# A decoder layer's last gather: waiting for the last block that holds rows, and the last normalisation on three engines

## What is computed

```python
x = _layernorm(x + _L0_attn_ref(x, ...), axis=-1)
x = _layernorm(x + _L0_xattn_ref(x, itok_BxS_13_99985, ctx_2048, ctx_2048, ctx_2048), axis=-1)
x = _layernorm(x + _L0_ffn_ref(x, ...), axis=-1)

def _L0_ffn_ref(x, gate_w, w_gate, w_up, w_down, sw_gate, sw_up, sw_down, expert_bias):   # E, K = 16, 2
    logits = flat @ gate_w.T
    probs = jax.nn.softmax(logits, axis=-1)
    _, top_idx = jax.lax.top_k(logits + expert_bias, K)
    top_w = jnp.take_along_axis(probs, top_idx, axis=-1)
    top_w = top_w / jnp.sum(top_w, axis=-1, keepdims=True)
    ...
    for e in range(E):
        out = out + combine[:, e:e + 1] * _swiglu(flat, w_gate[e], w_up[e], w_down[e])
    out = out + _swiglu(flat, sw_gate, sw_up, sw_down)
```

## Time and profile before

| | us |
|---|---|
| median of 3 runs | 677.91 |
| lowest, highest | 677.41, 678.26 |
| span of the profiled execution | 680.0 |
| mean granted TensorE clock | 0.971 |
| PE, DVE, ACT, POOL busy | 636.0, 531.8, 447.2, 475.5 |

### The profile page before, as it was taken

The page is one execution under the profiler, slowest core; times in us unless marked ns, Lnnn a source line. Parts: engine busy times, 40 slices in busy tenths (PEclk is TensorE's granted clock), DMA queues, the critical chain, the costliest instruction groups (busy, mean ns, idle before and its releaser), DMA issues.

```text
span 680.0 us, 11968 instructions
## 1 busy us (share of the span) xinstructions
PE 636.0 (94%) x3544; PEld 493.4 (73%) x3544; DVE 531.8 (78%) x849; ACT 447.2 (66%) x723; POOL 475.5 (70%) x452
## 2 busy tenths in 40 slices
PE   7999999999999999999999999999999999899920
PEld 6677887888878878888788788788898776455510
DVE  6999999999999999999999999859754539222236
ACT  3768788788787887887878879875324445333321
POOL 5395988789879887798798887586805817655244
PEclk9999999999999999999999999999999969999965
DMA  4231113113111131121111311133062780587324
GB/s 157 107 134 48 65 47 109 62 47 109 58 50 62 47 109 62 47 105 53 59 62 47 109 62 46 37 96 107 24 171 78 190 329 4 169 257 200 88 89 128
DMA packets 25896, 65.08 MB, mean 96 GB/s; under 512 B 4051, under 2 KB 16851, under 8 KB 23131
## 3 DMA queue, kind: packets, MB, share of 16 engines
q1 hardware_dynamic: 23035, 56.96, 25.2%
q0 software_dynamic: 2832, 7.75, 4.4%
HBM read 56.42 MB, written 8.28 MB: 95 GB/s over the span
## 4 chain that ended last, share of the span: by engine, by line
PE 68%; DVE 15%; issue 6%; ACT 5%; POOL 4%; DMA 2%; POOLq 0%; DVEq 0%; ACTq 0%
PE ps L835 27%; DVE conv L1662 8%; PE ps L865 7%; PE ps L849 5%; PE ps L1129 5%; PE ps L767 3%; PE ps L785 3%; ACT decay L1330 3%; PE ps L1173 3%; DVE decay L1646 3%; PE ps L850 2%; PE ps L809 2%; POOL conv L706 2%; PE ps L1103 1%; PE ps L874 1%
## 5 line engine op out<-in xcount | busy, mean ns | idle before, releaser
L1662 DVE SCALAR_TENSOR_TENSOR conv<-ps,w_raw,conv 128x506 f32<-128x506 f32 (+3 forms) x352 | 320.9, 935 | 12.1 <-ACT conv L1324 7.2
L835 PE MATMUL ps<-x_hi,w_hi 128*128 128x512 f32 x384 | 158.1, 412 | 3.8 <-DVE conv L1662 2.0
L835 PE MATMUL ps<-x_hi,w_lo 128*128 128x512 f32 x384 | 151.1, 393 | 0.0
L835 PE MATMUL ps<-x_lo,w_hi 128*128 128x512 f32 x384 | 150.0, 391 | 0.0
L1324 ACT ACTIVATE conv<-ps,w_raw 128x512 f32<-128x512 f32 x160 | 108.1, 686 | 61.4 <-PE ps L835 61.2
L498 POOL TENSOR_TENSOR decay<-cum_b,cum_tok 128x512 f32<-128x512 f32 (+1 forms) x128 | 103.2, 828 | 9.0 <-DMA cum_b<-cum_scratch 9.0
L835 PEld LDWEIGHTS ps<-x_hi,w_hi 128*128 128x128 f32 x384 | 72.2, 188 | 21.4 <-DVE conv L1662 3.5
L504 POOL TENSOR_TENSOR decay<-decay,mask 128x512 f32<-128x512 f32 x64 | 82.4, 1288 | 5.0
L835 PEld LDWEIGHTS ps<-x_hi,w_lo 128*128 128x128 f32 x384 | 72.0, 188 | 16.8 <-DVE w_lo L1588 0.2
L849 PE MATMUL ps<-conv 128*128 128x256 f32 x256 | 79.6, 393 | 2.3 <-DVE xs L1637 0.4
L835 PEld LDWEIGHTS ps<-x_lo,w_hi 128*128 128x128 f32 x384 | 72.4, 189 | 12.7
(11 more groups left out here) (263 smaller groups left out, 1101.6 us busy)
## 6 DMA issues: line engine op xcount, KB each, us to landing
cum_b<-cum_scratch SPq DMA_DIRECT2D x16, 1024.0 KB, 4.7
w_raw<-in_winT SPq DMA_DIRECT2D x15, 778.0 KB, 4.3
y_all<-in_wgu SPq DMA_DIRECT2D x4, 1408.0 KB, 11.6
late<-in_wdn SPq DMA_DIRECT2D x2, 1408.0 KB
x_scratch<-conv SPq DMA_DIRECT2D x19, 128.0 KB, 4.6
late<-in_woutT SPq DMA_DIRECT2D x1, 2048.0 KB, 8.3
ys_scratch<-y_blk SPq DMA_DIRECT2D x32, 64.0 KB
res_scratch<-conv SPq DMA_DIRECT2D x11, 130.0 KB
```

The costliest lines, as they stand in the source:

```text
L835: mm = pe.matmul(ps[:, tile_bank(n, tile) + hf, :], wp[:, par, w], xp[:, kk, t], start=(i == 0), stop=(i == 5))
L1662: dve.scalar_tensor_tensor(out=o[:, :, s:], in0=u[:, :, 0:T - s], scalar=w_raw[:, par, c:c + 1], in1=o[:, :, s:], op0=ALU.mult, op1=ALU.ad ...
```

## The change

Six things change together.

- The tail's gathers are cut in four parts, in this order: first pick of tiles 0 to 2; second pick of tiles 0 and 1; first pick of tiles 3 to 7; second pick of tiles 2 to 7. In round 22 (`SEEN_AT`) DVE works out for each part the last block that holds one of its rows. PE turns that [128, 4] table in round 24 behind the transposes' wait of item 23, DVE takes its maximum and writes four numbers.
- SP waits for each store to land, block after block, and counts `y_seen` up (`landed`). For blocks 0 to 8 it does that after it has issued block 8's store. Before each part POOL loads the part's number into a register, waits for `y_seen` against it, and does a one-column sum.
- POOL's `gather_block` runs up to seven blocks ahead from block 16 on, and the residual gathers come after blocks 7 to 14.
- The weight copies move to other places in memory, so that the gathered rows' place is free early. One wait of SP goes. `ys_dram` is filled once, early, from `x` (three transfers, 1.5 MB).
- ACT makes the exponentials of the picks in round 25, between two table loads. DVE makes the weights in round 27, and does `weigh_low` of tiles 0 to 2 before `gate_block` of the last item. ACT takes the last two `take_hidden`.
- The last normalisation is done by ACT for tiles 0 to 2, by POOL for 3 to 5 (after its last gather), by DVE for 6 and 7 (after its last statistics). The weighted sums are made in place in `y_of`, so a tile no longer waits for the normalisation of the one two before.

```diff
+PICK_PARTS = ((0, 0, HOISTED), (1, 0, LEADING), (0, HOISTED, TB), (1, LEADING, TB))   # HOISTED, LEADING = 3, 2
@@ SP, early
             load_cum(1, 1)
+            for lo, hi in YS_SET:
+                sp.dma_start(ys_dram[lo * G:hi * G, :], x[0:(hi - lo) * G, :]).then_inc(S["ys_set"], 16)
@@ SP, expert loop
+            def landed(j):
+                sp.wait_ge(st_y[j % NW], stored(j))
+                sp.sem_inc(S["y_seen"], 1)
             for j in range(NBLK):
                 store_block(j)
                 if 1 <= j <= NCOPY:
                     load_copy(j - 1)
+                if j == NCOPY + 1:
+                    for d in range(j):
+                        landed(d)
+                if j > NCOPY:
+                    landed(j)
@@ POOL
-                if j >= AHEAD:
+                if j >= NBLK - NX:
+                    pool.wait_ge(S["tx_done"], j - NX + 1)
+                elif j >= AHEAD:
                     pool.wait_ge(S["tx_done"], j - AHEAD + 1)
-                if j >= 9 and j % 2 == 1 and j < 9 + 2 * TB:
-                    gather_res((j - 9) // 2)
+                if 7 <= j < 7 + TB:
+                    gather_res(j - 7)
+            pool.wait_ge(S["v_lb"], 1)
+            for n, (k, lo, hi) in enumerate(PICK_PARTS):
+                pool.wait_ge(S["y_seen"], pool.value_load(last_blk[n:n + 1, 0:1], min_val=1, max_val=NBLK))
+                pool.tensor_tensor(part_seen[:, n:n + 1], zero[:, :], zero[:, :], ALU.add)
+                for b in range(lo, hi):
+                    gather_row(k, b)
+            for b in range(LAST_ACT, LAST_POOL):
+                pool.wait_ge(S["q2"], b + 1)
+                pool.tensor_scalar(o_tok[:, b, :], y_of[:, 0, b, :], ln_m2[:, b, 0:1], ln_v2[:, 1, b:b + 1],
+                                   ALU.subtract, ALU.mult).then_inc(S["n2p"], 1)
@@ ACT
+                if i == PICK_AT:
+                    act.preload_act_table_set("natural_log_exp_and_others")
+                    act.wait_ge(S["ld_res"], 16 * TB)
+                    act.activation(e_pick, res_tok[:, :, D + 2:D + 4].rearrange("p b k -> p k b"), ACT.Exp).then_inc(S["a_el"], 1)
+                    act.preload_act_table_set("silu_and_others")
@@ DVE
+            for i in range(TBS, ITEMS):
+                if i == ITEMS - 1:
+                    for b in range(HOISTED):
+                        weigh_low(b)
+                gate_block(i)
+                if TBS < i < ITEMS - 1:
                     take_hidden(i - 1)
+                if i == SEEN_AT:
+                    blocks_of_picks()
+                if i == PICK_AT + 2:
+                    weights_of_picks()
             for b in range(TB):
+                weigh_high(b)
+                if b + HOISTED < TB:
+                    weigh_low(b + HOISTED)
+                if b == TB - 1:
+                    for c in range(LAST_POOL, TB):
+                        last_norm(c)
@@ DVE, new functions
+            def blocks_of_picks():
+                dve.wait_ge(S["ld_res"], 16 * TB)
+                vlink(dve.tensor_copy(slot_t.rearrange("p (k b) -> p k b", k=PICKS),
+                                      res_tok[:, :, D:D + 2].rearrange("p b k -> p k b")))
+                vlink(dve.tensor_scalar(seen_a, slot_t, 6, NE - 1, ALU.logical_shift_right, ALU.bitwise_and),
+                      dve.tensor_scalar(seen_b, slot_t, 7, None, ALU.logical_shift_right))
+                vlink(dve.scalar_tensor_tensor(out=seen_c, in0=seen_b, scalar=float(NE), in1=seen_b, op0=ALU.is_ge, op1=ALU.mult))
+                vlink(dve.tensor_tensor(seen_f.rearrange("p k b -> p (k b)"), seen_a, seen_c, ALU.max))
+                for n, (k, lo, hi) in enumerate(PICK_PARTS):
+                    dve.tensor_reduce(part_f[:, n:n + 1], seen_f[:, k, lo:hi], AX.X, ALU.max).then_inc(S["v_blk"], 1)
+            def weigh_high(b):
+                r = y_of[:, 0, b, :]
+                dve.wait_ge(ld_y[b], 16 if b < HOISTED else 32)
+                dve.wait_ge(S["v_mix"], b + 1)
+                vlink(dve.scalar_tensor_tensor(out=r, in0=y_of[:, 1, b, :], scalar=w_pick[:, 1, b:b + 1], in1=r, op0=ALU.mult, op1=ALU.add))
+                vlink(dve.bn_stats(ln_s[:, b % 2, :], r))
+                dve.bn_aggr(ln_m2[:, b, :], ln_s[:, b % 2, :]).then_inc(S["s2"], 1)
```

More of the change, by code:

```diff
@@ L217, in build_layer @@
         slot_t = take(PICKS * TB).bitcast(I32)
+        seen_a, seen_b, seen_c = (take(PICKS * TB).bitcast(I32) for _ in range(3))
+        seen_f = take(PICKS * TB).rearrange("p (k b) -> p k b", k=PICKS)
+        part_f, part_seen, part_top = (take(NPART) for _ in range(3))
+        last_blk = take(1).bitcast(I32)
         e_pick, w_pick = (take(PICKS * TB).rearrange("p (k b) -> p k b", k=PICKS) for _ in range(2))
@@ L1148, in turn_hidden @@
                     pe.wait_ge(S["v_ht"], i - 1 - TBS)
+                if i == SEEN_AT + 1:
+                    pe.wait_ge(S["v_blk"], NPART)
+                    pe.transpose(ps[0:NPART, i % 2, 2 * P:3 * P], part_f, ident[:, :])
                 for c in range(2):
@@ L1156, in down @@
                     pe.wait_ge(S["a_ht"], i + 1)
-                else:
+                elif i < ITEMS - 2:
                     pe.wait_ge(S["v_ht"], i - TBS + 1)
@@ L1160, in down @@
                         pe.wait_ge(S["ld_dn"], 32)
+                else:
+                    pe.wait_ge(S["a_ht"], TBS + i - (ITEMS - 2) + 1)
                 if i >= 2:
@@ L1561, in _ @@
                     take_y(TBS - 1)
-                if i - 2 >= TBS:
+                if i < ITEMS and i - 2 >= TBS:
+                    take_y(i - 2)
+                if i >= ITEMS:
+                    take_hidden(i - 2)
+                    if i == ITEMS:
+                        act.preload_act_table_set("natural_log_exp_and_others")
                     take_y(i - 2)
@@ L1760, in rlink @@
-            def rlink(*group):
-                for ins in group:
-                    made[0] += 1
-                    ins.then_inc(S["v_rt"], 1)
-                dve.wait_ge(S["v_rt"], made[0])
+                if b < HOISTED:
+                    dve.wait_ge(ld_row[NX + b], 32)
+                else:
+                    dve.wait_ge(ld_y[b], 32)
+                dve.scalar_tensor_tensor(out=y_of[:, 0, b, :], in0=y_of[:, 0, b, :], scalar=w_pick[:, 0, b:b + 1],
+                                         in1=res_tok[:, b, 0:D], op0=ALU.mult, op1=ALU.add).then_inc(S["v_mix"], 1)
@@ L1893, in _ @@
                 dve.wait_ge(S["a_lg"], c + 1)
-                rlink(dve.tensor_tensor(biased[:, lo:hi, 0:NE], logit[:, lo:hi, :],
+                vlink(dve.tensor_tensor(biased[:, lo:hi, 0:NE], logit[:, lo:hi, :],
                                         eb_sb.unsqueeze(1).broadcast_to([P, n, NE]), ALU.add))
-                rlink(*[dve.max(top8[:, b, :], biased[:, b, 0:NE]) for b in range(lo, hi)])
-                rlink(dve.memset(top8[:, lo:hi, 2:8], PAD))
-                rlink(*[dve.match_replace(out=taken[:, b, :], in_to_replace=top8[:, b, :],
+                vlink(*[dve.max(top8[:, b, :], biased[:, b, 0:NE]) for b in range(lo, hi)])
+                vlink(dve.memset(top8[:, lo:hi, 2:8], PAD))
+                vlink(*[dve.match_replace(out=taken[:, b, :], in_to_replace=top8[:, b, :],
                                           in_values=biased[:, b, :], imm_value=HIT) for b in range(lo, hi)])
@@ L1973, in take_hidden @@
                                 ).then_inc(S["v_ht"], 1)
-            for i in range(TBS, ITEMS + 1):
-                if i < ITEMS:
-                    gate_block(i)
-                if i > TBS:
-                    take_hidden(i - 1)
-                if i == ITEMS - 2:
-                    dve.wait_ge(S["ld_res"], 16 * TB)
-                    dve.tensor_copy(slot_t.rearrange("p (k b) -> p k b", k=PICKS),
-                                    res_tok[:, :, D:D + 2].rearrange("p b k -> p k b")).then_inc(S["v_slot"], 1)
```

239 lines of the change are left out of this document (119 added, 120 removed).

## The result

The changed kernel took 684.46 us (median of 7 runs, 681.87 to 690.24) beside 678.19 us of the kernel before on the same chip: a ratio of 1.0107, with an interval of 1.0079 to 1.0134. It is slower by 6.3 us, where 671.2 us was predicted. The profiled execution took 690.24 us with a span of 688.4 us.

The account below looks back on a forecast made before the run. Bound: a tail of some 28 us without matmuls, POOL's gathers waiting for blocks 0 to 22. First gather 643.4, last 665.45, last L1739 669.0, plus 2.17 and 2.15: span 673.3, 6.7 off, median 671.2 us; range 662.0 to 676.0.

Parts of the forecast that it names:

- the one on the other engines: Edits on ACT, DVE and PE in rounds 22 to 25: PE held 1.5 us together, at no cost to the total.
- PE's holds: ACT's table loads in round 25 and DVE's blocks_of_picks in round 22 each hold PE 0 to 2 us.
- the cover: PE's later end, 653, lies under the tail gathers, so its holds and extra 0.2 us transpose cost nothing.
- Rival 4: The predicted mechanism with the early copy or PE's holds on top: 674 to 677 us; chance 0.08.
- the 0.92 against slower: Odds on the whole result: faster 0.90, same 0.02, slower 0.08.
- SP late for block 15: SP's store rounds of 2.4 us count block 15 at 642.7; first tail gather at 643.4 instead of 652.30.
- Rival 2: SP's store rounds outlast the block period: 691 us, slower from a round of 3.35 us on; chance 0.05.
- The parts' chain: POOL's tail gathers: 1.1 us between parts, three times; last gather 22.05 us after the first, at 665.45.
- DVE's chain: DVE's tail sums: fourth part's gathers from 659.2, last L1739 counterpart at 669.0, last normalisation at 671.2.
- The end behind DVE: From DVE's last normalisation to the span's end, the output transfer: 2.15 us as before.
- POOL's norms: Three normalisations behind POOL's last gather, at most 1.23 us each, done at 670.1 ahead of DVE's; late at 2 us.
- The sum: Whole kernel: span 680.0 to 673.3, 6.7 us off, taken off the 677.9 median to give 671.2 us.

Follow-up runs that it names:

- without the run ahead: Changed kernel with POOL's gathers of blocks 16 to 23 waiting for TensorE as before: 673.21 us, 671.77 and 680.22 us on other chips.
- SP counting one block behind: Changed kernel with POOL's run-ahead taken out and SP counting block j-1 landed behind the store of block j: 679.71 us.
- the thinned kernel: Changed kernel, no run-ahead, SP counting block j-1 behind block j's store, residual and tail gathers spaced out: 670.35 us, ratio 0.9871.
- six gathers: Kernel before plus six back-to-back POOL gathers that nothing reads, behind its last residual gather: 677.79 us on the first chip, 684.46 us on the sixth.
- the run ahead alone: Kernel before with only the rule letting POOL's gathers of blocks 16 to 23 run ahead: 694.34 us (ratio 1.0229), 690.39 us on another chip.
- the tail without early gathers: Changed kernel, every tail part waiting for all 24 blocks, first three sums behind DVE's loop: 687.81 us, 688.40 us on another chip.

## Why the prediction was wrong

**The step that failed** is the one on the other engines: PE's holds "costs nothing, because SP's counting does not wait for PE", and "PE's end moves to 653, under the gathers". PE's end moved to 674.2. Two things were missed. The extra and earlier gathers were priced as load on the DMA engines only, 0.42 us each, from the earlier trace rows; what they did to TensorE's counts had no price, and the trace of before could show none, as it has three gathers to two blocks. And the cover was read from the gathers' side. It fails on ACT's and DVE's side: the tail's sums and norms stand behind the last blocks in those queues, even where these blocks hold no rows. A line for the cover should have said from what point a late TensorE shows. The traces give it: the end is 13.8 us behind block 23's eviction once that is late, and 672.3 where it is not, so the cover ends at 672.3 - 13.8 = 658.5, and 674.61 is 16.1 us beyond it. Rival 4 (674 to 677) named PE's holds but was far too small, and still faster than before; no rival had this mechanism, and the 0.92 against slower was unfounded. What holds the counts, and why on some chips only, stays open.

**SP late for block 15: near the mark by luck.** Predicted first gather 643.4, measured 642.65, and 640.41 without the run ahead. But there SP sends block 9 at 618.21, where the working has nine blocks counted at 625.9. Of these 7.7 us some 4.9 are the lower clock in the profile that the prediction started from. And the six rounds from there to block 15's store at 637.44 take 3.2 us each, 2.6 to 4.6, and not 2.4 (3.0 in the changed kernel, 620.58 to 638.48). The shortest are 2.6 us; the landings there are 1.9 us at least, where 1.68 was taken. The Trainium skill's figure that the prediction set beside its row (DMA: Bandwidth & Descriptors, Anatomy of one DMA), with a round of 2.8 us by it, is given there for transfers of GpSimd, and these stores are SP's. With SP counting one block behind, its 16 transfers take 16.77 us, and the first tail gather stands at 632.70 in the thinned kernel.

**Rival 2** named 3.35 us as the round from which it is slower. The rounds were 3.2 us on average in the kernel without the run ahead, near that point, and it was still 4.6 us faster than before: the point was reckoned from a start at block 8 that was too late.

**The parts' chain: over-priced.** The step from part to part was to cost 1.1 us, three times. From 642.93 to 644.25 it is 1.32 instead of 1.25 us: 0.07. The register is loaded beside the gather still running. The last gather started 19.1 us after the first, not 22.05.

**DVE's chain: under-priced by 3.3 us.** Without the run ahead the fourth part's gathers start at 653.17, 6.0 us earlier than the 659.2 worked out, but DVE's last norm ends at 668.44, only 2.8 us ahead of the 671.2. "DVE is through with tiles 0 and 1 by then" did not hold. DVE's order is sum of tile 0, first sum of tile 3, sum of tile 1, and `weigh_low` of a tile from 3 on waits for both of its picks (`ld_y[b]` at 32). So DVE stood from 648.24 until tile 3's second pick had landed, with tile 1 behind it:

```profile
657.48 0.48 DVE L1772 SCALAR_TENSOR_TENSOR conv<-conv,y_all 128x256 f32<-128x256 f32 x1 [9.23 <-DMA conv<-ys_scratch,y_all]
```

No run has another order here. The end behind DVE was taken as before, 2.15 us, and is 3.9. POOL's norms were held for free at up to 2 us each; at 1.22 us they are indeed ahead of DVE's last, and still set the end (last section).

**The sum.** On the two chips where close gathers do nothing the kernel without the run ahead gave 672.3 and 670.9 of span against 673.3 predicted, and 673.2 and 671.8 us against 671.2. That it comes so near is luck: 673.3 was worked out from a profile that is 4.5 us longer than an execution at the median. The gain itself is 4.6 and 6.2 us where 6.7 was predicted. In the trace of the first chip the terms part from the working so: the first gather 3.0 us and the parts 3.0 us below it, DVE's chain 3.3 and the end 1.7 us above it (673.3 becomes 672.3). The changed kernel itself was measured five times, 684.5 to 688.6 us, each time with late counts. What it takes on a chip of the first sort is open.

## What to carry to other kernels

Price a gather of GpSimd that is pulled forward not only by its bytes but by what stands beside it: three gathers to two TensorE blocks showed no late count in any trace, two to a block did once even in the thinned version (2.9 us of waiting), and rows 1.25 us apart cost 6.3 us (six gathers) to 16.6 us (the run ahead alone) on some chips. When work is pulled off a late engine, look in each other engine's queue for what stands ahead of the work that it feeds; a block without rows still holds ACT and DVE. Compare a profile's span and clock with those of the runs before you take times from it. And measure on more than one chip before you give a cause to an edit: seven measurements pointed at the run ahead, against SP's later count alone, and only the same program on another chip showed what it was.

## What the runs showed of the hardware

**Close gathers and TensorE's counts.** On four of the six chips on which the experiments ran, and never on the other two, counts of TensorE reached ACT, DVE and POOL from 1.8 us (590.96 in the thinned kernel) to 15.8 us (661.81 on the fourth chip) behind the records of its matmuls while gathers stood close together, mostly 1.25 us apart, and then several at once. Behind a long row the last of them came 2.65 to 3.4 us after its last gather had started (622.34, 640.40, 661.81 and 627.48 in four traces). The traces also hold fewer records of semaphore updates on these four chips, 4,990 to 5,107 where the other two have 6,218 to 6,252, whatever the kernel. The profile of before has 5,082 and no late count, so missing records alone don't make one, but the mark "remote" may come from them; the idle times don't. Whether the matmuls themselves ran late or only their counts is open, as is the path that they share with the gathers, and why a chip has it. The Trainium skill (DMA: Bandwidth & Descriptors, Latency and other measured facts) guesses at port contention by the descriptor rings of GpSimd's transfers, for two of the DMA engines; no run here shows whether that is related.

**What follows POOL's last instruction.** In each kernel with norms on POOL the span ends 5.1 to 5.2 us after POOL's last instruction: 667.15 to 672.3, 662.2 to 667.4, 683.3 to 688.4, and 680.7 to 685.8 in the tail without early gathers. Before, POOL's last gather was over at 671.99 and 5.1 us behind it lay under DVE's work. By this reading three norms on POOL, ready ahead of DVE's last, still make the end about 1.7 us later. It is read from the traces only: moving them off POOL in the thinned kernel was not tried.
